# Cross-attention kernel on one core: new order of the first loads, of steps 4 and 6, and of the last column blocks

## The reference: what is computed

```python
text = encoder_hidden_states[:, :end_pos]        # 69 tokens
ip_h = encoder_hidden_states[:, end_pos:]        # 4 dummy + 4 image tokens
q = _split_heads(hidden_states @ w_q, HEADS)
k = _split_heads(text @ w_k, HEADS)
v = _split_heads(text @ w_v, HEADS)
out_text = _merge_heads(_sdpa(q, k, v))
mask_ip = _ip_mask(bbox, B, S, hidden_states.dtype)
k_ip = _split_heads(ip_h @ w_k_ip, HEADS)
v_ip = _split_heads(ip_h @ w_v_ip, HEADS)
out_ip = _merge_heads(_sdpa(q, k_ip, v_ip, mask=mask_ip))
out = out_text + IP_SCALE * out_ip
out = out @ w_out + b_out
out = out + residual
```

## Time and profile before

| | us |
|---|---|
| median of three runs | 403.87 |
| lowest, highest | 403.3, 404.85 |
| the profiled execution | 404.16 |
| its span, first to last instruction | 402.3 |
| DVE busy in it | 336.9 (84%) |
| ACT busy | 129.1 (32%) |
| POOL busy | 156.1 (39%) |
| DMA, mean | 181 GB/s |

### The profile page before, as it was taken

How to read it: one execution, slowest core, us unless ns; L and a number is a source line. 1 busy time by engine, 2 the same in 40 slices (tenths; PEclk the granted TensorE clock), 3 DMA queues, 4 the chain that set the end, 5 groups by cost and what they waited for, 6 DMA issues and landing times.

```text
span 402.3 us, 10795 instructions
## 1 busy us (share of the span) xinstructions
PE 393.6 (98%) x4452; PEld 292.3 (73%) x4452; DVE 336.9 (84%) x458; ACT 129.1 (32%) x196; POOL 156.1 (39%) x128
## 2 busy tenths in 40 slices
PE   8899999999999999999999999999999999999995
PEld 7688868577777776777777767777777677776773
DVE  4559779898899998998998999999989999999503
ACT  5236334453333322432323322343223322321100
POOL 0336622687326433364226442462227532222200
PEclk9999999999999999999999999999999999999998
DMA  8999736576657454764457454664466544544555
GB/s 280 382 374 333 206 78 233 158 232 171 182 158 223 132 139 138 196 190 138 137 168 231 124 148 135 209 172 145 121 211 193 142 131 127 156 124 119 178 158 182
DMA packets 42849, 72.96 MB, mean 181 GB/s; under 512 B 10544, under 2 KB 10672, under 8 KB 42800
## 3 DMA queue, kind: packets, MB, share of 16 engines
q1 hardware_dynamic: 37680, 67.02, 54.6%
q10 hardware_dynamic: 5120, 5.25, 5.2%
HBM read 35.53 MB, written 10.49 MB: 114 GB/s over the span
## 4 chain that ended last, share of the span: by engine, by line
PE 86%; DVE 3%; SPq 3%; DMA 3%; ACT 2%; issue 1%; ACTq 1%; DVEq 0%
PE ps L637 63%; PE ps L682 9%; PE ps L668 9%; PE ps L714 3%; SPq L259 2%; DMA wk_raw<-in_w_k 2%; ACT prob L395 1%; PE ps L720 1%; ACTq L403 1%; DVE text_max L501 1%; DVE prob L507 1%; ACT q L391 1%; DMA out_tiles<-res 1%; SPq L279 1%; DMA prob_k<-prob_t 1%
## 5 line engine op out<-in xcount | busy, mean ns | idle before, releaser
L357 POOL TENSOR_TENSOR prob<-prob,rden 128x1104 f32<-128x1104 f32 x40 | 82.2, 2056 | 200.5 <-DVE rden L530 200.5
L395 ACT ACTIVATE prob<-prob 128x1232 f32<-128x1232 f32 x40 | 50.0, 1250 | 65.7 <-DVE prob L518 65.7
L537 DVE STREAM_TRANSPOSE prob_t<-prob 128x1536 f32<-128x1536 f32 x40 | 70.7, 1767 | 0.2 <-POOL prob L359 0.2
L501 DVE TENSOR_REDUCE text_max<-ps 128x16 f32<-128x1104 f32 x40 | 52.1, 1303 | 17.1 <-PE ps L668 16.2
L637 PE MATMUL ps<-x_hi,wq_hi 128*128 128x512 f32 x200 | 59.2, 418 | 0.1
L637 PEld LDWEIGHTS ps<-x_hi,wq_hi 128*128 128x128 f32 x200 | 34.6, 188 | 33.9 <-issue 28.1
L525 DVE TENSOR_REDUCE den<-prob 128x16 f32<-128x1104 f32 x40 | 50.6, 1265 | 7.3 <-ACT prob L395 7.2
L438 ACT ACTIVATE o_hi<-ps 128x512 fp32r<-128x512 f32 x40 | 23.7, 592 | 101.9 <-PE ps L682 98.1
L637 PE MATMUL ps<-o_hi,wo_hi 128*128 128x512 f32 x200 | 55.6, 392 | 0.0
L637 PE MATMUL ps<-o_hi,wo_lo 128*128 128x512 f32 x200 | 55.1, 389 | 0.0
L637 PE MATMUL ps<-o_lo,wo_hi 128*128 128x512 f32 x200 | 55.1, 389 | 0.0
(11 more groups left out here) (58 smaller groups left out, 346.4 us busy)
## 6 DMA issues: line engine op xcount, KB each, us to landing
prob_k<-prob_t SPq DMA_DIRECT2D x320, 64.0 KB
stage<-in_x SPq DMA_DIRECT2D x38, 256.0 KB, 3.0
res<-in_x SPq DMA_DIRECT2D x37, 256.0 KB
out_tiles<-res SPq DMA_DIRECT2D x37, 256.0 KB, 2.2
prob_k<-prob_t ACTq DMA_DIRECT2D x160, 32.0 KB
wki_raw<-in_w_k_ip SPq DMA_DIRECT2D x5, 512.0 KB, 7.0
wk_raw<-in_w_k SPq DMA_DIRECT2D x5, 512.0 KB, 6.7
wv_raw<-in_w_v SPq DMA_DIRECT2D x5, 512.0 KB, 8.9
```

The source lines that it names most:

```text
L357: nc.gpsimd.tensor_tensor(e[:, :, 0:TEXT], e[:, :, 0:TEXT], rden[:, par, 0, :].unsqueeze(2).to_broadcast([P, QT * HG, TEXT]), ALU.mult)
L395: nc.scalar.activation(prob[:, c % 2, :, 0:TOKENS], prob[:, c % 2, :, 0:TOKENS], ACT.Exp).then_inc(exp_done, 1)
L501: nc.vector.tensor_reduce(text_max[:, par, :, :], s[:, :, :, 0:TEXT], AX_X, ALU.max).then_inc(text_max_done, 1)
L537: nc.vector.transpose(prob_t[:, c % 2, :, :, :].rearrange("p k n r -> p n k r"), prob[:, c % 2, :, :].rearrange("p n (k r) -> p n k r", r= ...
```

## The change

Loads: the context and K's text weights of unit 0 are loaded in two halves each (halves of the 1024 rows), ahead of w_q 0 and the first x tile; w_q 1 comes right behind x; V's first text weights come ahead of K's third; K's fourth ahead of V's second. TensorE's prologue warms up with 7 matmuls instead of 11, does K's text of unit 0 by halves, then Q 0, most of Q 1, image, rest of Q 1, fold, half of K's text 1, scores 0, the other half. Products of w_q wait for the high part first and for the low part where it is first used. ACT's and DVE's prologues follow: w_q 1 has its low part on DVE, exp(0) moves behind copy_k_part(2). Step 4 loads one block of w_out, step 5 the other. In step 6 (KD + 1) TensorE does make_o ahead of make_scores, and DVE does o_low ahead of shift_text. At the end all five last residuals go to `stage` (LATE = KD), and four column blocks instead of three are done by slices.

```diff
@@ -36,13 +36,13 @@
 TILES = SEQ // W
 UNITS = BATCH * TILES * KD
 AHEAD_Q, AHEAD_S = 2, 1
-LATE = KD - 2
+LATE = KD
 K_SLOTS, V_SLOTS, AHEAD_K = 2, 3, 2
 V_SLOT, V_ROUND = (0, 1, 2, 0, 2), (0, 0, 0, 1, 1)
 V_OLD = {3: 0, 4: 2}
 V_OLD_STEP = {V_OLD[g] + 1: g for g in V_OLD}
 X_JOBS = {0: (0, 1, 2), 1: (3, 4)}
-WO_JOBS = {4: (0, 1), 6: (2,), 7: (3,), 8: (4,)}
+WO_JOBS = {4: (0,), 5: (1,), 6: (2,), 7: (3,), 8: (4,)}
 BEHIND_OUT = KD + 1
 
 
@@ -120,7 +120,7 @@
         LAST_BANKS = [6, 0, 1, 2, 3]
 
 
-        WARM_BANK, WARM = 3, 11
+        WARM_BANK, WARM = 3, 7
         V_BANK, PART_COL = 6, 256
         K_BANKS = [5, 7, 5, 5, 5]
         K_PART_BANKS = [6, 7, 5, 5, 5]
@@ -137,7 +137,8 @@
         grid_loaded = sem("grid_loaded")
         eye_loaded = sem("eye_loaded")
         bias_loaded = sem("bias_loaded")
-        ctx_loaded = sem("ctx_loaded")
+        ctx_loaded = [sem(f"ctx_loaded{h}") for h in range(2)]
+        wk0_loaded = [sem(f"wk0_loaded{h}") for h in range(2)]
         wk_loaded = [sem(f"wk_loaded{s}") for s in range(K_SLOTS)]
         wki_loaded = [sem(f"wki_loaded{s}") for s in range(K_SLOTS)]
         wv_loaded = [sem(f"wv_loaded{s}") for s in range(V_SLOTS)]
@@ -274,29 +275,31 @@
                 sp.dma_start(out[c], out_tile(c)[0]).then_inc(stored[c % 2], 16)
 
             def prologue():
+                for half in range(2):
+                    kts = slice(KC // 2 * half, KC // 2 * half + KC // 2)
+                    sp.dma_start(ctx_sb[:, kts, :], ctx[:, kts, :]).then_inc(ctx_loaded[half], 16)
+                    sp.dma_start(wk_raw[:, 0, kts, :], w_k[0].rearrange("p (k n) -> p k n", n=P)[:, kts, :]).then_inc(wk0_loaded[half], 16)
                 load(("w_q", 0))
                 for kt in range(KD):
                     sp.dma_start(x0_raw[:, kt, :], x[kt]).then_inc(x0_loaded[kt], 16)
-                sp.dma_start(ctx_sb[:, :, :], ctx).then_inc(ctx_loaded, 16)
+                load(("w_q", 1))
                 load_k(0, wki_raw, w_k_ip, wki_loaded)
-                load_k(0, wk_raw, w_k, wk_loaded)
                 sp.dma_start(grid_sb[:, :], grid).then_inc(grid_loaded, 16)
                 sp.dma_start(box[:, :, :, :], bbox).then_inc(grid_loaded, 16)
                 sp.dma_start(eye_sb[:, :], eye).then_inc(eye_loaded, 16)
-                load(("w_q", 1))
                 load_k(1, wk_raw, w_k, wk_loaded)
                 load_k(1, wki_raw, w_k_ip, wki_loaded)
                 load(("w_q", 2))
+                load_v(0, wv_raw, w_v, wv_loaded)
                 load_k(2, wk_raw, w_k, wk_loaded)
                 load_k(2, wki_raw, w_k_ip, wki_loaded)
                 load(("w_q", 3))
-                load_v(0, wv_raw, w_v, wv_loaded)
                 load_v(0, wvi_raw, w_v_ip, wvi_loaded)
                 load(("w_q", 4))
+                load_k(3, wk_raw, w_k, wk_loaded)
+                load_k(3, wki_raw, w_k_ip, wki_loaded)
                 load_v(1, wv_raw, w_v, wv_loaded)
                 load_v(1, wvi_raw, w_v_ip, wvi_loaded)
-                load_k(3, wk_raw, w_k, wk_loaded)
-                load_k(3, wki_raw, w_k_ip, wki_loaded)
 
             def step(c):
                 if exists(c - BEHIND_OUT - 1):
@@ -345,9 +348,8 @@
                     nc.gpsimd.tensor_tensor(lo[:, n, :], slot, hi[:, n, :].bitcast(F32), ALU.subtract).then_inc(stage_lo, 1)
 
             def prologue():
-                pool.wait_ge(stage_lo, 1)
-                for g in range(1, 3):
-                    low(("w_q", g))
+                pool.wait_ge(stage_lo, 2)
+                low(("w_q", 2))
 
             def step(c):
                 par = c % 2
@@ -442,16 +444,16 @@
                 for kt in range(KD):
                     act.wait_ge(x0_loaded[kt], 16)
                     nc.scalar.activation(x_hi[:, 0, kt, :], x0_raw[:, kt, :], ACT.Copy).then_inc(x0_hi, 1)
+                high(("w_q", 1))
                 copy_q(0)
                 copy_k_part(0)
+                copy_q(1)
                 copy_k(0)
-                high(("w_q", 1))
                 high(("w_q", 2))
-                copy_q(1)
                 copy_k_part(1)
-                exp(0)
                 copy_k(1)
                 copy_k_part(2)
+                exp(0)
                 high(("w_q", 3))
 
             def step(c):
@@ -588,26 +590,32 @@
                 then(nc.vector.tensor_scalar(m[:, :, :, 0:DUMMY], any_in.unsqueeze(3).to_broadcast([P, BATCH, TILES * QT, DUMMY]),
                                              NEG, None, ALU.mult))
 
+            def w_q_low(g):
+                dve.wait_ge(stage_hi, g + 1)
+                nc.vector.tensor_tensor(wq_lo[:, g, :], stage[:, g, :], wq_hi[:, g, :].bitcast(F32),
+                                        ALU.subtract).then_inc(stage_lo, 1)
+
             def prologue():
                 nc.vector.memset(q[:, 0, 0:P], 0.0).then_inc(zeros_set, 1)
                 nc.vector.memset(prob[:, :, :, TOKENS:KEYS], 0.0)
-                dve.wait_ge(stage_hi, 1)
-                nc.vector.tensor_tensor(wq_lo[:, 0, :], stage[:, 0, :], wq_hi[:, 0, :].bitcast(F32),
-                                        ALU.subtract).then_inc(stage_lo, 1)
+                w_q_low(0)
                 for kt in range(KD):
                     dve.wait_ge(x0_hi, kt + 1)
                     nc.vector.tensor_tensor(x_lo[:, 0, kt, :], x0_raw[:, kt, :], x_hi[:, 0, kt, :].bitcast(F32),
                                             ALU.subtract).then_inc(x0_lo, 1)
+                w_q_low(1)
                 masks()
                 shift_text(0)
                 shift_img(0)
                 sums(0)
 
             def step(c):
+                if c == KD + 1:
+                    o_low(c - 2)
                 if exists(c + AHEAD_S):
                     shift_text(c + AHEAD_S)
                     shift_img(c + AHEAD_S)
-                if c > 2:
+                if c > 2 and c != KD + 1:
                     o_low(c - 2)
                 turn(c)
                 if exists(c + AHEAD_S):
@@ -644,10 +652,14 @@
                         if c >= 1:
                             pe.wait_ge(q_copied, c)
                         if c < KD:
-                            pe.wait_ge(stage_lo, NUMBER[("w_q", c)] + 1)
+                            pe.wait_ge(stage_hi, NUMBER[("w_q", c)] + 1)
                         elif g == 0:
                             pe.wait_ge(stage_lo, NUMBER[("x", c + KD - 1)] + 1)
                     if c == 0 and n % 3 == 0:
+                        pe.wait_ge(x0_hi, n // 3 + 1)
+                    if c < KD and n == (1 if c == 0 else KD):
+                        pe.wait_ge(stage_lo, NUMBER[("w_q", c)] + 1)
+                    if c == 0 and n % 3 == 2:
                         pe.wait_ge(x0_lo, n // 3 + 1)
                     last = product(Q_BANK, wq_hi, wq_lo, x_hi, x_lo, b, g, n, c > 0)
                     if n == 3 * KD - 1:
@@ -722,7 +734,11 @@
                 last.then_inc(made, 1)
 
             def k_text(g, kts=range(KC)):
-                pe.wait_ge(wk_loaded[g % K_SLOTS], 16 * (g // K_SLOTS + 1))
+                if g == 0:
+                    pe.wait_ge(ctx_loaded[kts[0] * 2 // KC], 16)
+                    pe.wait_ge(wk0_loaded[kts[0] * 2 // KC], 16)
+                else:
+                    pe.wait_ge(wk_loaded[g % K_SLOTS], 16 * ((g + 1) // K_SLOTS))
                 if g >= 2:
                     pe.wait_ge(k_copied, g if g > 2 else 1)
                 text_part(k_places[g], wk_raw[:, g % K_SLOTS, :, :], kts)
@@ -762,16 +778,17 @@
                 pe.wait_ge(zeros_set, 1)
                 for n in range(WARM):
                     nc.tensor.matmul(ps[:, WARM_BANK, 0:P], q[:, 0, 0:P], q[:, 0, 0:P], start=True, stop=True)
+                for half in range(2):
+                    k_text(0, range(KC // 2 * half, KC // 2 * half + KC // 2))
                 make_q(0, whole)
-                pe.wait_ge(ctx_loaded, 16)
+                make_q(1, whole[0:10])
                 k_image(0)
-                k_text(0)
+                make_q(1, whole[10:15])
                 k_fold(0)
+                k_text(1, range(0, KC // 2))
                 make_scores(0)
-                k_text(1)
-                make_q(1, whole[0:6])
+                k_text(1, range(KC // 2, KC))
                 k_image(1)
-                make_q(1, whole[6:15])
                 k_text(2)
                 k_fold(1)
                 k_image(2)
@@ -815,8 +832,12 @@
                 elif c >= UNITS - AHEAD_Q:
                     late_step(c)
                 else:
-                    make_scores(c + AHEAD_S)
-                    make_o(c - 2)
+                    if c == KD + 1:
+                        make_o(c - 2)
+                        make_scores(c + AHEAD_S)
+                    else:
+                        make_scores(c + AHEAD_S)
+                        make_o(c - 2)
                     make_q(c + AHEAD_Q, whole)
                     make_out(c - BEHIND_OUT)
 
@@ -824,15 +845,14 @@
```

(9 more changed lines are left out.)

## The result

The kernel after takes 411.1 us (median of six runs, 407.78 to 413.29) against 403.94 for the kernel before on the same chip: a ratio of 1.0171 over all executions of both, with a 95% interval of 1.0126 to 1.0216. It is slower, as forecast, but by 7 us instead of 2.2, and 2.8 us above the top of the range (408.3). The profiled execution of after took 407.78 us, the quickest of its six, so its trace shows less than the median does.

What follows compares the result with a forecast made beforehand. TensorE, busy 393.6 of 402.3 us, was taken as the bound, so shifts at its waits were summed: 1.8 + 2.0 - 1.6 = +2.2 us, set on the median of 403.87 for 406.1 us. Range 402.8 to 408.3.

Steps and rivals of the forecast that it cites:

- scores 1 start: Prologue: after the reordered loads and first Q, unit 1's scores start at 24.4, 0.5 before the old 24.90.
- scores 1 to 2: Prologue: exp(0), now behind copy_k_part(2), starts the 9.1 us chain later; TensorE waits, third scores at 34.0.
- lag at scores 2, kept until step 4: Prologue: third scores come 1.8 us later (range +1.2 to +2.5), and steps 1 to 3 win none back.
- steps 4 and 5, at make_q(8): One w_out block fewer and make_o(4) first bring TensorE 1.0 us earlier, swallowed by step 6's wait.
- scores 6 to 8: Step 6: o_low(4) ahead of unit 7's maxima delays the copy of q that scores 8 need: +2.0 us.
- the end, from make_o(37): End of kernel: one addition instead of three behind the last product, 0.2 of wait covered: -1.6 us.
- clock of TensorE: Whole kernel: the forecast sum had no clock term; a lower clock was only a rival, at the first Q.
- Nothing later in steps 1 to 3 has a gap that takes it back: Steps 1 to 3: the prologue's lag of +1.8 us stays whole.
- Step 6 free: Rival, step 6: o_high(4) ends by 80.8, so step 6 costs nothing; 403.1 us, chance 0.13.
- The prologue gains: Rival, prologue: scores 1 start below 22.8, so exp(0) is no later than before; 403.9 us, chance 0.12.
- The first Q at the lower clock level: Rival, prologue: after a shorter warm-up the 15 products run at half pace; +3, 409.1 us, chance 0.07.
- The end fails: Rival, end of kernel: the last residuals are late again, so the gain is missing; 407.7 us, chance 0.07.

Runs made afterwards that it cites:

- e1: The kernel after, unchanged, run again for a second trace and the spread: 411.17 us, ratio 1.0175 to the kernel before.
- e4: The kernel after with idle products, never read, in TensorE's waits (7 ahead of scores 2, 9 ahead of make_out(0), 7 behind it): 407.07 us, ratio 1.0073.
- e2: The kernel after with VectorE's old order in step 6 (maxima of unit 7 ahead of o_low(4)): 405.99 us, ratio 1.0052.
- e5: The kernel before with the new prologue alone (loads, K's text of unit 0 first, exp(0) behind copy_k_part(2)): 407.15 us, ratio 1.0076.
- e7: The kernel after with exp(0) back at its old place, behind copy_k_part(1) and ahead of copy_k(1): 407.68 us, ratio 1.0083.
- e14: The kernel after with both w_out blocks in step 4 again: 408.94 us, ratio 1.0123.
- e3: The kernel before with the new end alone (all five last residuals in own places, four column blocks by slices): 402.18 us, ratio 0.9956.
- e19: The kernel before with VectorE's swap of step 6 alone (o_low(4) ahead of the maxima of unit 7): 406.66 us, ratio 1.0073.
- e16: The kernel before with the new prologue, plus idle products (3 behind each half of K's text of unit 0, 8 ahead of scores 2): 407.49 us, ratio 1.0074.
- e13: The kernel before with the new end and TensorE's make_o(4) ahead of scores 7, both w_out blocks in step 4: 402.95 us, ratio 0.9957.
- e8: The kernel before with the new end, make_o(4) ahead of scores 7 and w_out 1 in step 5, VectorE's order old: 404.0 us, ratio 0.998.
- e6: The kernel before with both swaps of step 6 (make_o(4) first on TensorE, o_low(4) first on VectorE): 409.17 us, ratio 1.0112.

## Why the prediction came out as it did

| term | forecast | measured |
|---|---|---|
| scores 1 start | 24.4 | 24.57 |
| scores 1 to 2 | 9.6 (24.4 to 34.0) | 9.44 |
| lag at scores 2, kept until step 4 | +1.8, kept | +1.78, of it 1.20 kept at scores 6 |
| steps 4 and 5, at make_q(8) | -1.0, swallowed | -1.22, swallowed |
| scores 6 to 8 | +2.0 | +3.45 |
| scores 9 to make_o(37), no edit there | nothing | +0.7, of it 0.42 a wait for a DMA at 375.14 |
| the end, from make_o(37) | -1.6 | -1.75 |
| clock of TensorE | nothing | 1 to 7 us, some 4 at the median (from e1's line and e4) |

The rows but the last are of the profiled execution of after against that of before.

**Prologue: right, nearly to the row.** The chain was the one foreseen: exp(0) behind `copy_k_part(2)`, 9.1 us from it to the scores, TensorE waiting. The high part of w_q 0 was put at 7.9; it starts at 7.42 in the profiled execution and at 7.78 to 8.80 in e1, e2, e4, e5, e7 and e14. Scores 1 start at 25.01 to 26.41 in these six, against 24.64 to 25.54 with the old loads, so that they came at 24.57 is in part luck: the loads do not make them earlier in most traces. (The sum for the last low part of x also has a slip: 7.9 + 0.7 + 0.8 + 3.3 is 12.7.) One sentence was wrong: "Nothing later in steps 1 to 3 has a gap that takes it back". In before `make_o(0)`, at 50.62, takes 1.71 us for its eight pieces instead of the 1.06 of after, so scores 4 at 54.34 became only 55.44: 0.65 of the lag is absorbed there. That is a matter of the one execution: in e3 and e19, with the old prologue, `make_o(0)` takes 1.06 and 1.07 as well.

**Steps 4 and 5: right.** Lag 1.20 at scores 6, and `make_q(8)` at 80.40 against 80.42. Step 6's waits swallow it.

**Step 6: right mechanism, one term mis-sized.** The forecast had o_high(4) start at 82.8, on the assumption that ScalarE's x blocks start at 80.52 as before and w_out 1 adds 0.7. It starts at 85.72. Of the 2.9 us, 1.0 is that the DMA issues begin 1.0 later (78.91; what is left of the prologue's lag, which the sum has already), and 2.0 is that these four issues take 4.51 us instead of 2.49. The rest of the relay was right: from there to scores 8 it is 6.4 us, forecast 6.3 to 7.0, with L520 at its short value (0.29; the low part of w_out 1 on GpSimd was done at 89.47, before L520 at 90.00). The same four issues take 2.46 to 4.82 us in the traces of this study, so the 2.49 of before, the one row I had, was the short end of a spread. Where TensorE's order is the old one (before, e3, e5, e16, e19) they take 2.49 to 2.83; where make_o(4) goes first, up to 4.82 (e13). e13 against e3 differs in TensorE's swap alone and has 4.82 against 2.62, in one trace each; a cause isn't shown by that. The load of w_out 1 was a second term that I took for ready: in e1 and e8 it makes ScalarE wait 1.53 us.

**The end: right.** One addition, and -1.75 in the trace, -1.8 by the ratio of e3.

**The clock: the step that failed.** The forecast foresaw both waits of TensorE, of 2 to 3 us each, and priced them as waits only. It took up the clock in a rival, but at the first Q and for the shortened warm-up, with a chance of 0.07. Low stretches do occur there in some executions (0.50 from 10 to 12 us in e2 and e4) and cost less than the 3 us of that rival, because only four (e2) and eight (e4) of the 15 products run in them, 0.42 us apart instead of 0.23: from the first x_hi to the copy of q 0 it is 4.89 us in e5, 5.35 in e2, 6.17 in e4. The dearer ones lie behind the very waits that the change makes. There, in part of the executions, a wait that ends is followed by TensorE's work at half its rate: +1.45 us in e1 from scores 2 to 3, +3.0 from scores 8 to 9. Put in numbers: 406.9 at full clock, less the 404.0 of before, is +2.9, and the other 4.2 us of the median go to the clock. e4, which has the delays and nearly none of the low clock, gives the same: 407.07, 4.1 us less than after on that chip. Only the first is what I summed. The Trainium skill says on the page "TensorE: Matmul & The Clock Gate", section "What's actually happening", that "activity releases the throttle". I had read it for the warm-up alone; these traces agree with it in the middle of a kernel too, where waits are followed by the lower level (0.57 from 36 to 40 us and from 94 to 102 in e1), though not behind each wait of this length: behind 2.06 us at 34.01 in after, 2.10 at 34.58 in e5 and 2.04 at 34.45 in e14 the clock stays whole.

**Parts and whole.** Against before on their own chips, in the ratios above: prologue +0.76%, both swaps of step 6 +1.12% (e6), the split of w_out +0.5% (after against e14), the end -0.44%. The sum is +1.9%, measured +1.71%. No part is unaccounted for by more than the intervals. Taken out of after one at a time, the parts bring 5.2 (e2), 3.5 (e7) and 2.2 us (e14), 10.9 in all and more than the whole loss: they are not independent, as a part that goes takes its wait and a share of the low clock with it.

**The rivals.** Step 6 free: false, o_high(4) ended at 86.3 and not by 80.8. The prologue gains: false, scores 1 at 24.57. The first Q at the lower clock level: not in the profiled execution; in e2 and e4 it comes, at 0.5 to 1.3 us. The end fails: false.
